# State space: two products ahead of two scans, the second product written in place over the broadcast of B

## The reference, cut to what matters

```python
xc = silu(conv(x_in) + conv_b)                 # B, L, 256
xdbl = einsum('bld,de->ble', xc, W_xproj)      # step sizes, B, C
dt = softplus(einsum('blr,rd->bld', dt_r, W_dt) + b_dt)
def step(h, inp):                              # over the 128 tokens
    dt_t, B_t, C_t, u_t = inp
    dA = exp(dt_t[:, :, None] * A)
    h = h * dA + dt_t[:, :, None] * B_t[:, None, :] * u_t[:, :, None]
    y = einsum('bdn,bn->bd', h, C_t)
    return (h, y)
```

## Time and profile before

| | us |
|---|---|
| median of 3 runs (1925.93 to 1927.08) | 1926.71 |
| span of the profiled execution | 1948.6 |
| first product to last scan of the state space in that span | 707.7 to 1284.5 |
| mean granted TensorE clock | 0.916 |

### The profile page before, as it was taken

How to read it: one execution, slowest core, us unless ns; L and a number is a source line. 1 busy time by engine, 2 the same in 40 slices (tenths; PEclk the granted TensorE clock), 3 DMA queues, 4 the chain that set the end, 5 groups by cost and what they waited for, 6 DMA issues and landing times. The chain is left out here.

```text
span 1948.6 us, 31799 instructions
## 1 busy us (share of the span) xinstructions
PE 1562.9 (80%) x10219; PEld 1017.4 (52%) x10219; DVE 1491.3 (77%) x2947; ACT 953.5 (49%) x1491; POOL 920.7 (47%) x938
## 2 busy tenths in 40 slices
PE   8889888989699978977878878769998811699991
PEld 4545547988476632322333333236776611588891
DVE  6899986887488779999989999967777678533335
ACT  3545543575544567657656666436566410011114
POOL 4455442444200147677676677654344100366653
PEclk8999998999899989999988999979999855799996
DMA  4000000000000000000000000020000040466654
GB/s 144 2 0 0 0 1 27 2 2 1 12 1 0 1 1 1 1 1 0 0 1 0 0 0 1 1 78 11 5 9 5 3 145 0 159 209 206 212 171 135
DMA packets 49075, 75.34 MB, mean 39 GB/s; under 512 B 8861, under 2 KB 34821, under 8 KB 48437
## 3 DMA queue, kind: packets, MB, share of 16 engines
q1 hardware_dynamic: 43541, 64.12, 10.5%
q0 software_dynamic: 4544, 9.32, 1.6%
q10 hardware_dynamic: 864, 0.33, 0.1%
HBM read 62.26 MB, written 11.48 MB: 38 GB/s over the span
## 5 line engine op out<-in xcount | busy, mean ns | idle before, releaser
L1506 POOL TENSOR_TENSOR m_hC<-m_h,m_Cs 128x512 f32<-128x512 f32 x256 | 328.2, 1287 | 169.2 <-DVE m_h L1680 122.6
L1788 PE MATMUL PS<-m_hC,identf 128*128 128x512 f32 x512 | 296.5, 662 | 100.9 <-POOL m_hC L1506 99.9
L1680 DVE TENSOR_TENSOR_SCAN m_h<-m_dA,PS 128x512 f32<-128x512 f32 x256 | 312.4, 1220 | 11.2
L1788 PEld LDWEIGHTS PS<-m_hC,identf 128*128 128x128 f32 x512 | 93.0, 203 | 236.4 <-POOL m_hC L1506 208.9
L1675 DVE TENSOR_TENSOR PS<-PS,m_DU 128x512 f32<-128x512 f32 x256 | 178.4, 697 | 19.9 <-issue 3.8
L1616 ACT ACTIVATE m_dA<-m_DT,m_A 128x508 f32<-128x508 f32 x256 | 174.3, 714 | 31.3 <-DVE m_DT L1664 31.1
L1996 ACT ACTIVATE e_Sg<-PS 128x512 f32<-128x512 f32 x71 | 42.4, 597 | 223.0 <-PE PS L2238 178.8
L2238 PE MATMUL PS<-e_xT,e_WT 128*128 128x128 f32 x1136 | 143.8, 281 | 4.9 <-DVE e_xT L2146 3.4
L1608 ACT COPY m_Cs<-PS 128x512 f32<-128x512 f32 x128 | 73.7, 576 | 143.7 <-PE PS L1766 143.5
L2238 PEld LDWEIGHTS PS<-e_xT,e_WT 128*128 128x128 f32 x1136 | 135.4, 195 | 9.3 <-DVE e_xT L2146 7.1
L1935 POOL DMA_INDIRECT e_XG<-token_rows,e_ids x71 | 68.8, 969 | 138.9 <-DVE e_ids L2140 117.6
(11 more groups left out here) (411 smaller groups left out, 3801.6 us busy)
## 6 DMA issues: line engine op xcount, KB each, us to landing
e_WT<-in_w_wgu SPq DMA_DIRECT2D x71, 512.0 KB
token_rows<-X SPq DMA_DIRECT2D x2, 2048.0 KB
e_Y<-expert_rows SPq DMA_DIRECT2D x16, 256.0 KB, 4.0
k_BD<-in_w_bcr SPq DMA_DIRECT2D x1, 2464.0 KB, 9.5
e_w_wd<-in_w_wd SPq DMA_DIRECT2D x1, 2048.0 KB, 7.9
out_dram<-X SPq DMA_DIRECT2D x8, 256.0 KB, 2.4
X<-in_x SPq DMA_DIRECT2D x1, 1792.0 KB, 8.7
x_Cs<-in_ctx SPq DMA_DIRECT2D x8, 154.0 KB
```

What stands on the lines that cost most here:

```text
L1506: nc.gpsimd.tensor_tensor(hC[:, i % ND, :], hst[:, i % ND, :], Cs[:, n % ND, :], ALU.mult).then_inc(s["hC"], 1)
L1680: nc.vector.tensor_tensor_scan(hst[:, i % ND, :], dA[:, i % NA].rearrange("p b l -> p (b l)"), bank(4), 0.0, ALU.mult, ALU.add).then_inc(s ...
L1788: nc.tensor.matmul(bank(5 + ch), c.identf[:, :], hC[:, i % ND, :], start=False, stop=(n == NS - 1)).then_inc(s["yacc"], 1)
```

## The change

DVE's order for a state is now product, product, scan, scan. The product of ch 0 still goes to bank 4. That of ch 1 is written over the spread B(n) itself, in bank 1 or 2, and the scan of ch 1 reads it there. A product for ch 0 waits for the scan of ch 0 of the state before (bank 4), that for ch 1 (n above 0) waits for nothing, and the scans wait as before. `spread_b` of B(n) now waits for the second scan of state n - 2 in place of its products.

```diff
--- before.py
+++ after.py
@@ -1446,6 +1446,14 @@
 
         return bank((1 if isinstance(g, int) and g == 0 else 7, 0)[ch])
 
+    def spread_at(n):
+
+        return bank(1 + n % 2)
+
+    def inputs_at(n, ch):
+
+        return bank(4) if ch == 0 else spread_at(n)
+
     def split(stages):
 
         return {n: st for n, st in stages.items() if n in OPEN}
@@ -1664,20 +1672,26 @@
                     nc.vector.scalar_tensor_tensor(DT[:, par, ch, :], DT[:, par, ch, :], 0.0, L[:, ch, :], ALU.max, ALU.add).then_inc(s["dt"], 1)
                 return stage
 
-            def step(g, par, i, left):
+            def product(g, par, i):
                 n, ch = i // CH, i % CH
-                if i < CH:
+                if n == 0:
                     dve.wait_ge(s["du"], g * CH + i + 1)
                 if ch == 0:
                     dve.wait_ge(s["B"], g * NS + n + 1)
-                if not first(g, i, 1):
-                    dve.wait_ge(s["h"], g * NI + i)
-                nc.vector.tensor_tensor(bank(4), bank(1 + n % 2), DU[:, par, ch, :], ALU.mult).then_inc(s["dBu"], 1)
+                    if not first(g, i, CH):
+                        dve.wait_ge(s["h"], g * NI + i - 1)
+                nc.vector.tensor_tensor(inputs_at(n, ch), spread_at(n), DU[:, par, ch, :], ALU.mult).then_inc(s["dBu"], 1)
+
+            def step(g, par, i, left):
+                n, ch = i // CH, i % CH
+                if ch == 0:
+                    product(g, par, i)
+                    product(g, par, i + 1)
                 dve.wait_ge(s["dBu"], g * NI + i + 1)
                 dve.wait_ge(s["dA"], g * NI + i + 1)
                 if not first(g, i, ND):
                     dve.wait_ge(s["hC"], g * NI + i - ND + 1)
-                nc.vector.tensor_tensor_scan(hst[:, i % ND, :], dA[:, i % NA].rearrange("p b l -> p (b l)"), bank(4), 0.0, ALU.mult, ALU.add).then_inc(s["h"], 1)
+                nc.vector.tensor_tensor_scan(hst[:, i % ND, :], dA[:, i % NA].rearrange("p b l -> p (b l)"), inputs_at(n, ch), 0.0, ALU.mult, ALU.add).then_inc(s["h"], 1)
 
             def gate(g, par):
                 dve.wait_ge(s["yacc"], g * NI + NI)
@@ -1755,8 +1769,8 @@
                 if n == 0:
                     pe.wait_ge(s["lo"], g + 1)
                 if not first(g, n, 2):
-                    pe.wait_ge(s["dBu"], g * NI + CH * (n - 1))
-                nc.tensor.matmul(bank(1 + n % 2), W["sel"][:, n:n + 1].to_broadcast([96, P]), hi[:, par, :], start=True, stop=True).then_inc(s["B"], 1)
+                    pe.wait_ge(s["h"], g * NI + CH * (n - 1))
+                nc.tensor.matmul(spread_at(n), W["sel"][:, n:n + 1].to_broadcast([96, P]), hi[:, par, :], start=True, stop=True).then_inc(s["B"], 1)
 
             def spread_c(g, par, n):
                 if n == 0:
```

## The result

| | us |
|---|---|
| kernel before, median of 4 runs (1925.93 to 1929.99) | 1926.89 |
| changed kernel, median of 4 runs (1913.37 to 1917.12) | 1915.48 |
| ratio (95% interval) | 0.9941 (0.9929 to 0.9953) |
| the same pair, measured a second time: 1927.45 and 1913.21 | 0.9922 (0.9909 to 0.9936) |

The changed kernel is 11.4 us faster, 14.2 in the second measurement. The forecast was 1910.0, 16.8 us faster. The direction is right, the time lies in the range, and a third of the gain is missing by the first measurement, a sixth by the second.

A forecast was written before the change was run, and what follows sets the result against it. DVE bounds only the last group and gate to x0; elsewhere a relay of PE, ACT and POOL does. 7.9 + 6.9 + 0.8 + 1.2 = 16.8 us off 1926.7 gives 1909.9; range for 8 in 10: 1898 to 1922.

The forecast's parts named there:

- The last group, 7.9: Group preparing no successor: states at 3.48 us instead of 4.04, 8.1 us saved less 0.2 for queued hC.
- Gate to x0, 6.9 and 0.8: From a gate to PE's next first projection, DVE sets the time: 1.15 us saved six times, 0.8 in the first group.
- x0 to the second SiLU, 1.2: From PE's first projection to ACT's second SiLU, PE is full: 0.2 us saved in each of six groups.
- SiLU to gate: nothing: From ACT's second SiLU to the next gate, ACT then POOL hide DVE's gain: 0 us saved.
- relay: From x0 to the gate, PE, ACT and POOL are each full in turn, 53.55 us; DVE merely keeps pace.
- rival 4: Relay looser than thought: 1855 if DVE bounds everywhere, 1901 if only PE's half clock ahead of six gates vanished; together 8%.
- The moved waits: zero: spread_b's wait for a state's second scan ends before PE arrives there: 0 us, 13 us at most.
- rival 1: In-place product in bank 1 or 2 is dear: slower from 0.38 us extra each, 1932.8 at 0.52; 8%.
- Rival 2 (spacings stay): Each DVE instruction still waits for the last to leave in full: states keep 4.04 us, +5.1 us, 1931.8; 3%.
- Rival 3 (gaps close, nothing overlaps): DVE's gaps close without overlap: 3.84 us a state, the last group gains 3.0 us, 1923.7; 8%.
- E to the second DU: From ACT's last correction E to POOL's second DU: 14.31 us, recurring in seven groups within a few tenths but for one.
- The carry of 21.9 us: The median of the runs lies 21.9 us below the profiled span; this difference was carried over unchanged to the forecast.

The follow-up runs named there:

- less work in the relay: Softplus logarithm term computed on 8 of 512 columns only (ACT and POOL), in both kernels: 1913.31 us in the kernel before, 1879.61 in the changed kernel.
- The zero matmuls: Two bf16 matmuls of zeros added on PE ahead of each of steps 22 to 31: changed kernel 1899.69 us, kernel before 1924.92 us.
- the late broadcast alone: Kernel before with only spread_b changed, waiting for the second scan of state n - 2 instead of its second product: 1926.68 us, 0.9999.

## Why the prediction was right, and where it was not

- *A DVE instruction that need not wait for its predecessor starts before that one's recorded end.* Right, and the base of it all: 1.12 us from scan to scan and 0.59 for a product, forecast 1.13 and 0.61. With the waits put back, the new order has 4.05 for a state. By the rule weighed in the prediction, in the Trainium skill, VectorE: DVE Perf Modes, "The DRAIN you can't avoid", the run with the waits and the changed kernel would have taken the same time; the measurement decides against it here, 1934.59 against 1913.21. The same page's section "Two Vector instructions with no wait between them" allows the earlier start for an instruction that is not held back, and with that the traces agree.
- *The last group, 7.9.* It gave 9.9. States at 3.42 instead of 3.48 make 0.9 of the difference. The rest is behind the last scan: the gate waited 2.67 us for PE after and 3.51 before, where I had added 0.2 for a queue.
- *Gate to x0, 6.9 and 0.8.* Measured 6.3 in the six groups and 1.1 in the first. Right.
- *x0 to the second SiLU, 1.2.* Measured 1.1. Right.
- *SiLU to gate: nothing.* **This is the step that failed**, by 6.3 us. That the other engines hide DVE's gain there was right: with less work in the relay the changed kernel gains 33 us, the kernel before 13.8, so DVE does wait. But I took the relay's length as fixed because its instructions stay the same. It has PE in it, whose instructions have two durations. I saw the half clock ahead of the gate, 0.50 in the earlier trace rows, and used it only as a gain that might come in rival 4. The change made it worse instead: 0.71 to 0.74 in every tail, where it had been 0.74 to 1.00, and DU to gate 3.7 us longer. The zero matmuls show it for the 4.7 us between E and the gate: with the clock at 1.00 there they are back, and 6.3 more. The other 1.5, from SiLU to E, go with the clock in the traces alone.
- *The moved waits: zero.* Right for the kernel before, where the late broadcast alone gave 0.9999. In the changed kernel the wait can't be taken back by itself, as the second scan reads that bank; PE's loads wait 12.3 us for it in sum, 0.8 at most. How much of DVE's 25.7 us of waiting for the spread comes from that was not tested.
- *The product in place: no more than now.* Right, 0.67 to 0.70 us for each of the 256, which ends rival 1.
- *Rival 2 (spacings stay)* would have given 1931.8; it is the state of affairs in the run with the old waits, 1934.59. *Rival 3 (gaps close, nothing overlaps)* falls with the same spacings of 3.42. *Rival 4 (a looser relay)* falls: the seven groups are only 2.2 us shorter in sum. Its second half, 8 us more if PE's clock didn't drop, was of the right order (12 to 13.5 with the zero matmuls), only it had to be brought about.
- *E to the second DU* is said to recur within a few tenths but for one group. It is 14.29 to 14.31 us in all seven. *The carry of 21.9 us* from span to runs belonged to that one profiled execution (after the change the span, 1911.4, lies 2.0 below the 1913.37 of the same execution). The forecast in the runs' time took only the 16.8 off the median, so it is not touched.

The forecast on the numbers: 16.8, plus 1.5 where more was gained, less 6.3, is 12.0, beside 12.1 in the state space of the profiled executions and 11.4 and 14.2 in the runs.

Open: DVE waits twice for some 2 us, put down to issue, at the ends of the loop's turns, in both kernels; that wasn't tried. Nor was why PE was granted less clock after the change. What stands beside it in the traces is that PE's work comes in lumps. In the tail shown PE stood idle for 1.93 us ahead of 912.33 and was busy for 3.45 of the 6.30 us up to there, and by 912.33 it was at half clock; in the same tail before, its longest wait for an hC was 1.59. In the whole state space POOL waits for ACT's copies of C for 74.6 us, against 35.6 before, and PE's additions wait for POOL. Which of these waits matters was not tested.

## What to carry to other kernels

Where a chain on one engine alternates between dependent instructions, interleave two independent chains, so that no instruction waits for the one just ahead of it; a scratch buffer that one of them can overwrite in place may be all that this needs. Then ask of each stretch which engine sets its time, and when TensorE is in it, don't take its durations as given: look at the granted clock, and how its idle time will be cut up once the others run faster. When it drops in a stretch that matters, a few matmuls with zeros that wait for nothing cost little and gave nearly as much here (13.5 us) as the change itself (14.2 beside it); where another engine set the time, they gave 2.3.

## What the runs showed that I had not expected

- The worth of the fillers depends on who is next: the same twenty zero matmuls a group gave 13.5 us in one kernel and 2.3 in the other, with the same 5.2 us from DU to gate in both.
- The first softplus operation takes 1.74 us when it starts right behind its release, in each of the seven groups, and 0.74 at the least in the kernel before (means 1.618 after, 1.115 before). In the tail shown above it starts at 913.54, while POOL's hC runs from 913.46, and POOL's next operation takes 1.72 instead of 1.27. The two hold each other up. The Trainium skill, SBUF — State Buffer, "SBUF: two separate sides", says that a DVE instruction with two SBUF inputs and a GpSimd instruction that reads SBUF share one pair of ports, which whoever comes first keeps to its end; the two durations agree with it. DVE waits there anyway, but POOL's DU waits for the softplus in its turn, 3.8 us in six waits (0.6 in one before), and E to DU is 14.5 us instead of 14.3 in five groups. With the zero matmuls the second softplus takes 0.91 to 0.92 us and E to DU is at 14.3 again, while the first still takes 1.74. So I put at most that 1.0 us on it; no run took it away by itself.
